# A Mamba block and a mixture of experts on one Trainium2 core: convolution taps between scans, a table of projections by gap, B and C rows in column tiles

## What is computed

```python
xs, res = jnp.split(xn @ W_in, 2, axis=-1)            # 512 -> 2 x 1024 channels
xs = silu(depthwise_causal_conv(xs, conv_w, conv_b))  # 4 taps along time
xdbc = xs @ W_xp                                      # dt_r 128, B 16, C 16 columns
delta = softplus(dt_r @ W_dt + b_dt)
h = h * exp(delta * A) + delta * B * xs               # step by step, 16 states a channel
y = sum_n(h * C) + D * xs
out = (y * silu(res)) @ W_out + x
```

## Time and profile before

| | before |
|---|---|
| median of 3 runs | 1887.87 us (1887.38 to 1889.99) |
| the profiled execution's own time | 1889.72 us |
| its span | 1888.0 us |
| busy PE / DVE / ACT / POOL | 1608.2 / 1214.4 / 784.0 / 1127.6 us |
| first scan to last gate of the loop | about 82 to 1020 us |
| the stretch 1060 to 1888 us (experts) | PE 701.9, DVE 284.4, POOL 267.2 us busy |

### The profile page before, as it was taken

The page is one execution under the profiler, slowest core; times in us unless marked ns, Lnnn a source line. Parts: engine busy times, 40 slices in busy tenths (PEclk is TensorE's granted clock), DMA queues, the critical chain, the costliest instruction groups (busy, mean ns, idle before and its releaser), DMA issues. The chain is left out here.

```text
span 1888.0 us, 18202 instructions
## 1 busy us (share of the span) xinstructions
PE 1608.2 (85%) x4166; PEld 722.8 (38%) x4167; DVE 1214.4 (64%) x1723; ACT 784.0 (42%) x1271; POOL 1127.6 (60%) x695
## 2 busy tenths in 40 slices
PE   5679998899988899888788599992499999999995
PEld 2233433334333344333233245551244444444442
DVE  3599999999999999999996233317533333323331
ACT  4566576665666666565663134410011111111110
POOL 0299899998789998998986111100144444544443
PEclk9899999999999999999899799996599999999998
DMA  3600125101141111411000621210066677676663
GB/s 111 267 14 26 35 64 199 35 31 35 59 183 52 37 35 31 164 48 36 7 17 0 224 112 62 66 44 17 24 158 184 175 223 188 154 208 186 158 146 57
DMA packets 65359, 182.84 MB, mean 97 GB/s; under 512 B 10016, under 2 KB 14368, under 8 KB 56608
## 3 DMA queue, kind: packets, MB, share of 16 engines
q1 hardware_dynamic: 47232, 138.48, 20.8%
q0 software_dynamic: 18080, 43.82, 11.8%
HBM read 147.65 MB, written 34.62 MB: 97 GB/s over the span
## 5 line engine op out<-in xcount | busy, mean ns | idle before, releaser
L749 POOL TENSOR_TENSOR h<-h,c_rep 128x2048 f32<-128x2048 f32 x128 | 578.7, 4525 | 39.7 <-DVE h L650 34.7
L841 PE MATMUL bank<-h,ident 128*128 128x512 f32 x916 | 448.6, 633 | 87.8 <-POOL h L749 66.7
L495 ACT ACTIVATE bank<-delta,a_neg 128x512 f32<-128x512 f32 x512 | 336.8, 682 | 188.5 <-DVE h L650 187.2
L841 PEld LDWEIGHTS bank<-h,ident 128*128 128x128 f32 x916 | 180.3, 202 | 334.5 <-issue 215.5
L650 DVE TENSOR_TENSOR_SCAN h<-bank,state,h 128x512 f32<-128x512 f32 x256 | 305.9, 1257 | 0.0
L650 DVE TENSOR_TENSOR_SCAN h<-bank,h 128x512 f32<-128x512 f32 x256 | 290.6, 1198 | 0.6 <-ACT bank L495 0.6
L1568 PE MATMUL h_ps<-w_ring,xT 128*128 x640 | 285.3, 599 | 3.5 <-issue 3.5
L640 DVE TENSOR_TENSOR h<-bank,b_rep 128x2048 f32<-128x2048 f32 (+1 forms) x105 | 227.8, 2183 | 44.2 <-ACT bank L488 30.2
L1519 DVE TENSOR_TENSOR act<-gs,h_ps 128x256 f32<-128x256 f32 x80 | 33.7, 421 | 248.1 <-ACT gs L1492 248.1
L1492 ACT ACTIVATE gs<-h_ps 128x256 f32<-128x256 f32 x80 | 30.7, 384 | 380.5 <-PE h_ps L1568 380.5
L1568 PEld LDWEIGHTS h_ps<-w_ring,xT 128*128 128x128 f32 x640 | 120.8, 191 | 162.9 <-issue 162.9
(11 more groups left out here) (212 smaller groups left out, 1815.5 us busy)
## 6 DMA issues: line engine op xcount, KB each, us to landing
w_ring<-in_w SPq DMA_DIRECT2D x32, 1024.0 KB, 6.1
b_rep<-bcd SPq DMA_DIRECT2D x16, 1024.0 KB, 6.7
c_rep<-bcd SPq DMA_DIRECT2D x16, 1024.0 KB, 4.8
w_ring<-in_w SPq DMA_DIRECT2D x32, 512.0 KB, 8.4
w_in<-in_w_in_x SPq DMA_DIRECT2D x32, 256.0 KB, 2.6
w_res<-in_w_in_res SPq DMA_DIRECT2D x32, 256.0 KB, 2.7
xa<-in_x SPq DMA_DIRECT2D x20, 256.0 KB, 2.9
xb<-in_x SPq DMA_DIRECT2D x16, 256.0 KB, 2.7
```

The lines of the kernel that those rows point to most:

```text
L495: eng.activation(da[j][:], delta[:, g % 2], ACT.Exp, scale=a_neg[:, col:col + 1])\
L749: ins = eng.tensor_tensor(h[:, q], h[:, q], c_rep[:, Q * q:Q * q + Q, :], ALU.mult)
L841: ins = eng.matmul(y_ps[:], c.ident[:], h[:, q, j, :], start=False, stop=(q == NQ - 1 and j == Q - 1))
```

## The change

Five edits, all in the Mamba stage:

```diff
-        bc = sb("bc", [2 * NS, SEG])
+        bc = sb("bc", [P, P])
...
-            return g // DC < NSEG - 1 and g % DC in (3, 4, 5)
+            return g // DC < NSEG - 1 and g % DC in (3, 4, 5, 6)
...
-            for slot, gap in enumerate((0, 1, 3)):
-                n = 3 * d + slot
-                if n < len(order):
-                    gaps[gap].append(order[n])
...
+            plan = (([out(0, 0)], [out(0, 1), turn(1)], [out(1, 0)]),
+                    ([out(1, 1)], [out(2, 0), turn(2)], [out(2, 1)]),
+                    ([out(3, 0)], [out(3, 1), turn(3)], [into(0)]),
+                    ([into(1)], [into(2)], []),
+                    ([into(3)], [into(4)], [into(5)]),
+                    ([into(6)], [into(7)], []),
+                    (x_proj[:3], x_proj[3:], []),
+                    ([], [("turn", s + 2, 0, 0)], []))[d]
...
+            gaps = [plan[0], plan[1], [z], [dt] + plan[2]]
```

```diff
                 def tap(s, j):
...
+                    edge = 0 if s % 2 == 0 else KW - 1
+                    for t in range(edge):
+                        eng.activation(x[:, t:t + 1], ps[:, t:t + 1], ACT.Identity, scale=w, bias=tail[:, j, t:t + 1])
+                    eng.activation(x[:, edge:], ps[:, edge:], ACT.Identity, scale=w, bias=conv_b[:, j:j + 1])\
+                        .then_inc(S["tap_done"], 1)
...
-                    eng.activation(bc[:], ps[0:2 * NS, :], ACT.Copy).then_inc(taken, 1)
+                    eng.activation(bc[:], ps[:, 0:P], ACT.Copy).then_inc(taken, 1)
...
-                    eng.dma_start(dram.bcd[s], bc[:]).then_inc(S["bcd_written"], 16)
-                    eng.wait_ge(S["bcd_written"], (s + 1) * 16)
+                    for t in range(ST):
+                        eng.dma_start(dram.bcd[s, :, t * P:(t + 1) * P], bc[2 * NS * t:2 * NS * (t + 1), :])\
+                            .then_inc(S["bcd_written"], 16)
+                    eng.wait_ge(S["bcd_written"], (s + 1) * 16 * ST)
...
+                        for d in range(half * DC // 2, (half + 1) * DC // 2):
+                            for t in range(ST):
+                                ins = eng.matmul(out[2 * NS * t:2 * NS * (t + 1), 0:P], w_xp[:, d, DR:],
+                                                 xs[:, s % 2, d, t * P:(t + 1) * P], start=(d == 0), stop=(d == DC - 1))
```

```diff
-                    front(g - 1, 1)
                     spread(g, 1)
-                    scans(g, 0)
+                    scans(g, 0, front(g - 1, 1, 1))
...
-                    scans(g, 2)
-                    front(g - 1, 3)
+                    scans(g, 2, front(g - 1, 3, 2))
...
-                    scans(g, 3)
-                    front(g, 0)
+                    scans(g, 3, front(g, 0, 2))
```

More of the change, by code:

```diff
@@ L201, in gap_items @@
             s, d = divmod(g, DC)
[L202 to L205, removed]
-            for slot, gap in enumerate((0, 1, 3)):
-                n = 3 * d + slot
-                if n < len(order):
-                    gaps[gap].append(order[n])
[L210 to L215, removed]
+            out = lambda i, half: ("out", s - 1, i, half)
+            into = lambda j: ("in", s + 1, j, 0)
+            turn = lambda i: ("turn", s + 1, i, 0)
+            x_proj = [("bc", s + 1, 0, 0), ("bc", s + 1, 0, 1), ("dtr", s + 1, 0, 0), ("dtr", s + 1, 0, 1)]
+            plan = (([out(0, 0)], [out(0, 1), turn(1)], [out(1, 0)]),
[6 more added lines that the diff above has]
+                    ([], [("turn", s + 2, 0, 0)], []))[d]
+            z, dt = ("z", (g + 1) // DC, g + 1, 0), ("dt", (g + 2) // DC, g + 2, 0)
+            gaps = [plan[0], plan[1], [z], [dt] + plan[2]]
             return [[it for it in gap if 0 <= it[1] < NSEG] for gap in gaps]
@@ L533, in _ @@
                         tap(it[1], it[2])
-                    for it in gap_of(g - 1, 1, "bc", 1):
-                        bc_out(it[1])
+                    for it in gap_of(g - 1, 1, "dtr", 1):
+                        dtr_out(it[1])
                     if d == DC - 1 and s + 2 < NSEG:
@@ L558, in _ @@
                         tap(it[1], it[2])
+                    for it in gap_of(g, 0, "bc", 1):
+                        bc_out(it[1])
                     if d == DC - 1:
@@ L593, in link, with conv_steps, step @@
                     links[0] += 1
-                def conv(s, j):
-                    n = s * DC + j
-                    u, m = where["in", s, j]
+                    return links[0]
+                def conv_steps(s, j):
+                    u, _ = where["in", s, j]
                     p, x, w = work[u], xs[:, s % 2, j, :], conv_w
-                    eng.wait_ge(S["tap_done"], n + 1)
-                    for sft in range(1, KW):
+                    ends, mids = [], []
+                    def step(sft):
+                        if sft == 1:
+                            eng.wait_ge(S["tap_done"], s * DC + j + 1)
                         if s % 2 == 0:
@@ L613, in conv @@
                         if sft < KW - 1:
-                            link(ins)
-                            eng.wait_ge(S["conv_chain"], links[0])
-                    ins.then_inc(work_free[u], 1)
+                            mids.append(link(ins))
+                        else:
+                            ins.then_inc(work_free[u], 1)
+                    return [lambda sft=sft: step(sft) for sft in range(1, KW)]
                 def added(s, i):
@@ L622, in added, with front @@
                     eng.tensor_tensor(xb[:, n % 2], xb[:, n % 2], ps[:], ALU.add).then_inc(taken, 1)
[L624 to L628, removed]
+                def front(g, gap, at):
+                    steps = [step for it in gap_of(g, gap, "in") for step in conv_steps(it[1], it[2])]
+                    steps += [lambda it=it: added(it[1], it[2]) for it in gap_of(g, gap, "out", 1)]
+                    return {at + n: step for n, step in enumerate(steps)}
                 def spread(g, q):
@@ L641, in spread, with scans @@
                                       b_rep[:, Q * q + a:Q * q + b, :], ALU.mult).then_inc(S["bq_made"], 1)
-                def scans(g, q):
+                def scans(g, q, between={}):
                     s, d = divmod(g, DC)
@@ L651, in scans @@
                             .then_inc(S["scan_done"], 1)
+                    if Q in between:
+                        between[Q]()
                 def gate(g):
@@ L667, in _ @@
                 for j in range(DC):
-                    conv(0, j)
+                    for step in conv_steps(0, j):
+                        step()
                 spread(0, 0)
@@ L807, in run @@
                         for d in range(half * DC // 2, (half + 1) * DC // 2):
[L808 to L809 removed]
+                            for t in range(ST):
+                                ins = eng.matmul(out[2 * NS * t:2 * NS * (t + 1), 0:P], w_xp[:, d, DR:],
+                                                 xs[:, s % 2, d, t * P:(t + 1) * P], start=(d == 0), stop=(d == DC - 1))
+                        if half:
+                            ins.then_inc(work_full[u], 1)
+                    elif kind == "dtr":
+                        eng.wait_ge(S["xp_loaded"], 16)
+                        eng.wait_ge(S["xs_ready"], s * DC + (half + 1) * (DC // 2))
+                        for d in range(half * DC // 2, (half + 1) * DC // 2):
+                            ins = eng.matmul(out[:], w_xp[:, d, 0:DR], xs[:, s % 2, d, :], start=(d == 0), stop=(d == DC - 1))
                         if half:
```

23 lines of the change are left out of this document (11 added, 12 removed).

## The result

The changed kernel is slower: median 1898.59 us (1892.46 to 1900.61) against 1889.35 us (1883.06 to 1894.64), eight runs each; ratio 1.0044, 95% interval 1.0027 to 1.0062, beyond what can be told from no change. I had forecast 1875 in a range of 1867 to 1890. The profiled execution took 1900.49 us (before 1889.72), its span 1898.8 us (before 1888.0).

A forecast was written before the change was run, and what follows sets the result against it. DVE was taken to set most Mamba-loop blocks, POOL and PE close behind. From 1889.72 us, -8.7 - 10.1 + 1.5 + 6.2 - 1.8 = -12.9 gave 1876.8, as a median 1875, range 1867 to 1890.

The forecast's parts named there:

- Edge columns by ScalarE: Small tap instructions moved to ACT: mostly hidden by its idle time except at gap 0; 1.5 us cost in all.
- New table and bc: PE's chain from the gate of d = 6 to the next segment: segment ends move later, 6.2 us cost in all.
- X: PE's time for both halves of bc, 7.2 us before; taken as 3.5, each us moving the total by 3.5.
- rival A: Full overlap of bc's column groups on PE: X = 1.75, 6.1 us less, 1869 us; chance 0.16.
- Waits that go by the new places: DVE's waits for PE's last out item (9.8 us) and for taps (3.5) go; 10.1 us saved net.
- Taps between scans: Convolution steps placed between DVE's scans: 0.50 us saved per odd-segment convolution, 0.25 per even; 8.7 us in all.
- B product, fourth dense slot: In d = 6 DVE saves 1.08 us; POOL's 2.35 more falls in its idle time and costs nothing there.
- Opening: Before the loop, the second half of bc on the path shortens: 1.8 us saved up to DVE's start.
- C: Slower, on PE from the gate of d = 6 to its last sum: X = 8.3 plus gap 0 tap waits, 1895; chance 0.13.
- D: POOL sets blocks 3 to 5, so the 8.7 us of DVE savings vanish: 1884 us; chance 0.10.

The follow-up runs named there:

- The filler: Changed kernel with the dt matmul written five times in d = 3 and 5 of segments 0 to 2, same result: ratio 0.9988.
- the moved gap 0: Changed kernel with the steps of gap 0 run behind the four scans of quarter 3, not from place 2 on: ratio 0.9982.
- the run with the split gap: Changed kernel with d = 6 projections split two and two, both bc halves in gap 0 and both dtr halves in gap 1: ratio 1.0043.
- the run with the places alone: Kernel before with only the steps moved between scans (places 1, 2 and 2), edge instruction kept on DVE: ratio 0.9963.
- the old list: Changed kernel with the list of projections and ScalarE's bc and dtr copies as before, the other edits kept: ratio 0.9912.
- the run with both remedies: Changed kernel with dt written six times (nine in segment 1) in d = 3 and 5, and gap 0's steps behind quarter 3: ratio 0.9944.

## Why the prediction was wrong

**The step that failed** is "Edge columns by ScalarE", where it says of gap 0: "In these ACT has one decay, of about a tap's length, and the tap, 0.77 + 0.77 + 0.6 = 2.1 us: it just fits." That step followed the tap back to ACT alone. The tap also needs PE's in item, and that stands behind gate, D term and sum: in block 4 PE's D term starts 12.8 us behind the first scan, the in item ends 11.1 us later, at 23.8, and the step is due at 20.0. Four scans of cover had hidden this; two do not. I priced it at 1.5 us; the taps' waits at gap 0 are 17.1 us, and another 6.9 stand at gap 3, where I had counted none (before: 3.8 in all). The filler and the moved gap 0 took 11 and 12 us off, and 19 together. For d = 3 to 7 the sum had -8.7 + 1.5 + 6.2 = -1.0 us; these stretches measured 23.6 more.

**The clock was no term of the sum at all.** I read the empty gaps as relief for PE. With two of them ahead of a gate that comes later, PE's waits for the gate rose from 16.9 to 45.4 us, and the clock fell behind all six in d = 4 and 6. The prediction even had the row for it: PE idle 1.43 us ahead of the D term while the half of dtr was still in front of it; with that half (3.7) gone and the gate 1.0 later, 6.1 us of idling could have been added up from numbers in the text; it became 7.34.

**New table and bc.** X is 1.95 us, not 3.5, near the 1.75 of rival A. By the Trainium skill, TensorEngine Tiling (Array Packing), section Key Properties, different tiles load weights and multiply in parallel, and this trace agrees (64 instructions in 1.95 us). With 1.95 the same sum gives 1869.6, further from the measured time: the table's 6.2 us were too much for bc and had nothing for what follows. The move of the gate was also right in direction (+1.0 expected; in block 14 PE's D term, which follows it, starts 15.0 us behind the first scan, before 13.7). Two things in the same stretch were missed: DVE's second product waits for the sum of quarter 1 (3.44, 3.64 and 1.70 us at the end of d = 6), a wait that the run with the split gap only moved on, and the D term and sum ahead of it are slow (3.1 us in block 14). The sign given for this part did not come: DVE's idle time at the three segment starts is 10.1 us after 9.3, not 2 to 5 us more each, and POOL's longest wait for PE's sum in d = 7 is 2.23 us, not 5, since DVE had already waited.

**Waits that go by the new places:** right for the out items. 10.1 expected; the leaving blocks gave 11.3, the out item's wait fell from 9.8 to 1.0, and the run with the places alone was 7 us faster with its taps' waits in it. The 3.5 us of taps at gap 1 went too, but other taps wait now.

**Taps between scans:** right in size. In block 4 a body starts at 222.08 and the scan behind it at 222.72, 0.64 us later; expected 0.66. A convolution of an odd segment saves 0.24 + 0.29 = 0.53 us; expected 0.50. What was saved in this way did not reach the end of these blocks.

**B product, fourth dense slot:** too small for these runs to tell, as the run without it shows.

**Opening:** 1.3 us for 1.8, and by the measured X it should have been 2.6. It cannot be told: kernels with the same opening as the changed one start their first scan between 78.9 and 81.0 us, and those with the old bc at 80.0, 81.8 and, the kernel before, 82.3.

**The rivals.** C had the right sign and a price near enough (1895), but that was luck: most of it came from an X of 8.3 where X was 1.95, and the taps, put at 0.4 to 0.5 us each at gap 0, waited 17.1 us in all there, up to 5.35 at a time. The sign given for a wrong forecast (DVE waits for taps by more than 0.5 us each) did appear. D (POOL sets blocks 3 to 5) did not occur; in block 4 it was the chain over PE.

## What to carry to other kernels

Before an instruction is moved earlier in one engine's order, follow every input back to the engine that starts the chain, not to the one that hands it over: here a tap came from ACT but hung on DVE's own gate, through PE. A list of work by gap should keep an engine busy ahead of its longest wait; a gap emptied there costs twice if that engine's clock falls with idling, as PE's did here. And price a rearrangement one edit at a time: four edits of the five, with the old list, were worth 0.9%, and the list cost 1.3%.

## What the runs showed of the hardware

Float32 matmuls of 32 weight columns and 128 moving columns, written to four groups of 32 partitions in turn, start in fours: in block 14 the four starts of a group lie within 0.02 us, and from group to group it is 0.109 us, the pace at which single 128-column instructions follow each other. Both instructions of each matmul are in that count, so four run side by side throughout, and 64 take 1.95 us. It is not the narrower weights: with the same 32 weight columns and 512 moving ones before, eight took 3.62 us, 0.43 apart or 0.108 for each 128 columns. The change from full to tiled matmuls and back costs about 0.1 us each way: behind the sum that starts at 507.78 in the run with both remedies the tiled group starts 3.53 us later, where a full group starts after 3.43, and the first full instruction behind the tiles takes 0.70 us for 0.59. Behind an idle time of 4.9 us the next ten PE instructions took 7.6 us, behind 1.47 us they took 4.6 (block 4, without and with the filler), the granted clock over 205 to 215 us being 0.66 and 1.00. An engine can thus be made faster by giving it more to do: eight needless instructions of 0.43 us brought 3.1 us back in block 4.
